# Two units of scores, then two units of weighing V, on TensorE

## The chip, the core and the metric

The kernel runs on one core of one Trainium2 chip. The metric is the device time in microseconds; before the change the median of three runs is 332.66 us (327.57 to 334.11).

## The reference

A gated cross-attention block followed by a gated feed-forward block with low-rank experts, in float32, on 32 images (batch entries) of 128 rows and width 128:

```
q = layernorm(x) * 8**-0.5;  k, v = split(ctx_2048, 2)       # 16 heads of 8
w = softmax(q @ k.T + b + mask(seq_len))                     # 128 x 128 per head
x = x + tanh(g_xattn) * (w @ v)
h = layernorm(x)
gate_e = (times e is in the top 2) * (sum of the top 2 scores)
x = x + tanh(g_ffn) * sum_e gate_e * (relu(h @ wi.T + bi + (h @ A_e.T) @ B_e.T) @ wo.T + bo)
```

The change concerns the attention alone. What has to be done there for each image: the scores of 16 heads, the row maxima, the exponentials, and the weighing of V with the sums of the rows.

## The kernel before

**Units.** An image's 16 heads are four units of four heads (c = 0 to 3). The scores are computed twice. First with queries as rows (line 779), so that VectorE can reduce them to negated row maxima (row_max, line 1040). Then with keys as rows (line 785), where the negated maximum comes in as one more row of the contraction, so that ScalarE can take the exponential of what is in the bank (exps, line 594). Q and K are split into bfloat16 parts which lie, with bias and maximum rows, in a tensor called stack, 64 partitions for each half of the heads. A call scores(m, n, c) issues four matmuls of each kind, interleaved, on different halves of the array: first-kind scores of image m, second-kind scores of image n.

**The pipeline.** All four engines run a loop over q (turns, or pairs of images), i (0 or 1) and c. At a turn, m = 2q+i and n = 2(q-2)+i: the second scores are four images behind the first. weigh_v (line 807) multiplies V by the probabilities in float32, four heads in four column groups of 32 of the array, eight matmul records a unit; behind(j) calls it for unit j. Its output bank o_acc is copied out by ScalarE (copy_o, line 600) when an image's four units are done, transposed by TensorE (transpose_o, line 817), and normalised and added to X by VectorE (add_attention, lines 1076 to 1089).

**The maxima.** The 32 columns of negated maxima of a pair are split on VectorE into three bfloat16 parts (split_max, lines 1054 to 1063, in four steps), transposed (transpose_max, 795), copied by ScalarE (copy_max, 606) and written to the stack by a DMA that ScalarE issues (max_to_stack, 611). The pair's second scores begin in the turn after the one that transposes them.

**Q and K of the pair q+3.** GpSimd permutes K (446) and normalises X (456); TensorE transposes both into one bank (transpose_k 751, transpose_q 756); ScalarE makes the first part (first_part, 579) and a float copy (float_copy, 583); GpSimd takes the rest (480); ScalarE makes the second part (second_part, 587); GpSimd the third (484); SyncE's DMAs bring them to the stack.

**What sets the order.** Each engine's order is written out by hand; semaphores join them. The waits that matter here:

```
scores:   pe.wait_ge(s_max, i - 1)       # two banks of first scores
scores:   pe.wait_ge(s_maxrow[p % 4], ...)   # line 773, first unit of a pair: the maxima's DMA
scores:   pe.wait_ge(s_exp, k - 1)       # two banks of second scores
weigh_v:  pe.wait_ge(s_oc, n)            # line 803, c == 0: copy_o of image n-1
weigh_v:  pe.wait_ge(s_exp, i + 1)
copy_o:   act.wait_ge(s_pv, CH * (n + 1))    # all four units of image n weighed
exps:     act.wait_ge(s_pv, i - 3)       # four buffers of probabilities
```

In the turns from q=13 to 15 the place of Q and K is taken by transposes and copies of the weights (lines 731 to 741, 569, 572). From q=16 there are only second scores; the layer norms of the feed-forward part (normalise(g), line 620, four activations each) and its gates run between them. Then comes the feed-forward stage, one group of four images at a time.

Of the kernel before, what the change touches and what calls it, by code (L numbers as in the profile page):

```python
# [39 lines left out]
def flamingo(nc, x, ctx, seq_len, g_xattn, g_ffn, b, wi, bi, wo, bo, lora_a, lora_b, gate_w, gate_b, out):  # L40
    B, S, D = x.shape
# [5 lines left out]
    PAIRS = B // 2  # L47
# [4 lines left out]
    CH = 4  # L52
# [7 lines left out]
    with es:  # L60
# [184 lines left out]
        LEAD = 4  # L245
# [313 lines left out]
        def _(act):  # L559
# [21 lines left out]
            def float_copy(p):  # L581
                act.wait_ge(s_rest, p)
                act.activation(full[:, :], qk_t[:, :], ACT.Copy).then_inc(s_full, 1)  # L583
# [5 lines left out]
            def exps(n, c):  # L589
                i = CH * n + c  # L590
                act.wait_ge(s_sc2, i + 1)
                if i >= 4:
                    act.wait_ge(s_pv, i - 3)
                act.activation(probs[:, i % 4, :], sc2[i % 2][:, :], ACT.Exp).then_inc(s_exp, 1)  # L594
# [7 lines left out]
            def copy_max(p):  # L602
                act.wait_ge(s_mT, p + 1)
                if p >= 2:
                    act.wait_ge(s_maxrow[(p - 2) % 4], 16 * ((p - 2) // 4 + 1))
                act.activation(max_rows[:, p % 2, :], bank_max[:, 0:256], ACT.Copy).then_inc(s_mTc, 1)

            def max_to_stack(p):
                act.wait_ge(s_mTc, p + 1)
                c0 = 256 * (p % 2)  # L610
                act.dma_start(stack[MAX_ROW:MAX_ROW + STEP * (ROWS - 1) + 1:STEP, (p // 2) % SLOTS, :, c0:c0 + 256],
                              max_rows[:, p % 2, :]).then_inc(s_maxrow[p % 4], 16)
# [47 lines left out]
            for q in range(PAIRS + 3):  # L660
                for i in range(2):
                    n = 2 * (q - 2) + i
                    for c in range(CH):
                        if 0 <= n < B:
                            exps(n, c)
                        if c == 1 and 0 <= n - 1 < B:
                            copy_o(n - 1)
                        if i == 0:
                            if c == 2 and LEAD <= q + 3 < PAIRS:
                                first_part(q + 3)  # L670
                            if c == 3 and 0 <= q - 1 < PAIRS:
                                copy_max(q - 1)
                            if c == 3 and LEAD <= q + 3 < PAIRS:
                                float_copy(q + 3)
                        else:
                            if c == 0 and 0 <= q - 1 < PAIRS:
                                max_to_stack(q - 1)
                            if c == 2 and LEAD <= q + 3 < PAIRS:
                                second_part(q + 3)
                        if c == 3 and 0 <= 2 * (q - WEIGHTS_AT) + i < 4:  # L680
                            copy_weights(2 * (q - WEIGHTS_AT) + i)

                        at = (q - PAIRS, i, c)
                        if at == (0, 0, 3):
                            normalise(0)
                        if at == (0, 1, 2):
                            copy_xT(0)
                        if at == (1, 0, 0):
                            gate_exp(0)
                        if at == (1, 0, 1):  # L690
                            normalise(1)
                        if at == (1, 1, 1):
                            copy_xT(1)
                        if at == (1, 1, 2):
                            x_high(0)
                        if at == (2, 0, 1):
                            normalise(2)
# [22 lines left out]
        def _(pe):  # L720
# [23 lines left out]
            def transpose_k(p):  # L744
                pe.wait_ge(s_kperm, 2 * (p + 1))
                if p > LEAD:
                    pe.wait_ge(s_full, p - LEAD)
                elif p >= 1:
                    pe.wait_ge(s_rest, p)
                for i in range(2):  # L750
                    pe.transpose(qk_t[:, 256 + i * 128:256 + (i + 1) * 128], kperm[:, p % 2, i, :], ident[:, :])  # L751
# [7 lines left out]
            def scores(m, n, c):  # L759

                first, second = 0 <= m < B, 0 <= n < B
                if first:
                    i, Q, s = CH * m + c, m // 4, (m // 4) % SLOTS
                    if c == 0 and m % 4 == 0:
                        pe.wait_ge(s_stack[s], 16 * STACK_DMAS * (Q // SLOTS + 1))
                        if Q < SLOTS:
                            pe.wait_ge(s_fixed[s], 32)
                    if i >= 2:
                        pe.wait_ge(s_max, i - 1)
                if second:  # L770
                    k, p = CH * n + c, n // 2
                    if c == 0 and n % 2 == 0:
                        pe.wait_ge(s_maxrow[p % 4], 16 * (p // 4 + 1))
                    if k >= 2:
                        pe.wait_ge(s_exp, k - 1)
                for j in range(G):
                    if first:
                        (at, h0), q0 = score_rows(UNITS1[c]), (m % 4) * 128
                        mm = pe.matmul(sc1[i % 2][:, j * 128:(j + 1) * 128], stack[at, s, h0 + j, q0:q0 + 128],  # L779
                                       stack[at, s, h0 + j, 512 + q0:640 + q0], start=True, stop=True)  # L780
                        if j == G - 1:
                            mm.then_inc(s_sc1, 1)
                    if second:
                        (at, h0), q0, t = score_rows(UNITS2[c]), (n % 4) * 128, (n // 4) % SLOTS
                        mm = pe.matmul(sc2[k % 2][:, j * 128:(j + 1) * 128], stack[at, t, h0 + j, 512 + q0:640 + q0],  # L785
                                       stack[at, t, h0 + j, q0:q0 + 128], start=True, stop=True)
                        if j == G - 1:
                            mm.then_inc(s_sc2, 1)

            def transpose_max(p):  # L790
                pe.wait_ge(s_msplit, NMS * (p + 1))
                if p >= 1:
                    pe.wait_ge(s_mTc, p)
                for i in range(2):
                    mm = pe.transpose(bank_max[:, i * 128:(i + 1) * 128], max_part[:, p % 2, i, :], identb[:, :])  # L795
                mm.then_inc(s_mT, 1)
# [15 lines left out]
            def transpose_o(n):  # L812
                pe.wait_ge(s_oc, n + 1)
                if n >= 1:
                    pe.wait_ge(s_norm, NNORM * (n - 1) + 4)
                for i in range(2):
                    mm = pe.transpose(o_t[:, i * 128:(i + 1) * 128], o_rows[:, n % 2, i * 128:(i + 1) * 128], ident[:, :])  # L817
                mm.then_inc(s_oT, 1)
# [77 lines left out]
            def behind(j):  # L896
                if 0 <= j < CH * B:
                    weigh_v(j // CH, j % CH)
# [5 lines left out]
            for q in range(PAIRS + 3):  # L904
                for i in range(2):
                    m, n = 2 * q + i, 2 * (q - 2) + i
                    for c in range(CH):
                        if c == 3:
                            behind(CH * n)
                        scores(m, n, c)  # L910
                        if i == 0:
                            if c == 0 and LEAD <= q + 3 < PAIRS:
                                transpose_k(q + 3)
                            if c == 2 and LEAD <= q + 3 < PAIRS:
                                transpose_q(q + 3)
                        if c == 3 and 0 <= n - 1 < B:
                            transpose_o(n - 1)

                        if c != 2:
                            behind(CH * n + c - 2)  # L920
                        if i == 0 and c == 1 and 0 <= q - 1 < PAIRS:
                            transpose_max(q - 1)
                        if c == 2 and 0 <= 2 * (q - WEIGHTS_AT) + i < 5:
                            transpose_weights(2 * (q - WEIGHTS_AT) + i)

                        at = (q - PAIRS, i, c)
                        if at == (0, 1, 1):
                            transpose_x(0)
                        if at == (0, 1, 3):
                            lora_and_gates(0)  # L930
                        if at == (1, 1, 0):
                            transpose_x(1)
# [411 lines left out]
```

## Time and profile before

| | |
|---|---|
| median of three runs | 332.66 us |
| the profiled execution | 328.71 us, span 326.8 us |
| TensorE busy | 260.8 us (80%) |
| VectorE busy | 236.8 us (72%) |
| ScalarE busy | 165.1 us (51%) |
| GpSimd busy | 124.1 us (38%) |
| mean granted clock of TensorE | 0.963 |
| the chain that ended last, by engine | PE 34%, issue 20%, DVE 20%, DMA 10% |

PE is TensorE, DVE VectorE, ACT ScalarE, POOL GpSimd, SP SyncE. The attention loop with both kinds of scores runs from about 43 to 182 us, the feed-forward stage from about 207 us to the end. A granted clock of 1.00 is 2.4 GHz, 0.50 is 1.2 GHz.

### The profile page before, as it was taken

The numbers are of one execution on the slowest core, as the hardware profiler recorded it, in microseconds if no ns is written. First come the engines' busy times: TensorE is split into PE (matmuls) and PEld (weight loads), VectorE is DVE, ScalarE is ACT, GpSimd is POOL, SyncE is SP. The second block draws the span as 40 slices with busy tenths as digits, with TensorE's granted clock in tenths as the row PEclk, the third lists the DMA queues.
The fourth block names the chain that finished last, engine by engine and source line by source line (L and its number), as shares of the span: only waits on it lengthen the run. The fifth ranks groups of instructions, "written<-read, shape, count | busy, mean of one in ns | idle before, by whom it ended". The sixth has DMA issues, their size and how long they took to land.

```text
span 326.8 us, 8070 instructions
## 1 busy us (share of the span) xinstructions
PE 260.8 (80%) x2934; PEld 179.0 (55%) x2934; DVE 236.8 (72%) x810; ACT 165.1 (51%) x332; POOL 124.1 (38%) x240
## 2 busy tenths in 40 slices
PE   0222058979879698889899886999999999999894
PEld 0111034444445344445455454878888888888764
DVE  1862078788969678869988778688797978867431
ACT  1230004767858577768776886444443445333230
POOL 9963005465536656534211412050504325033120
PEclk9999999997979869979999998799999999999999
DMA  6789980874908479682600000001010100101011
GB/s 172 141 181 189 233 155 10 197 143 106 231 12 227 78 181 193 117 168 62 165 9 4 19 2 1 2 1 32 2 32 2 33 10 24 32 2 34 0 34 32
DMA packets 36615, 26.70 MB, mean 82 GB/s; under 512 B 7992, under 2 KB 34400, under 8 KB 36576
## 3 DMA queue, kind: packets, MB, share of 16 engines
q1 hardware_dynamic: 33792, 25.12, 34.9%
q10 hardware_dynamic: 2784, 1.07, 1.5%
q8 instruction: 24, 0.39, 0.5%
q14 instruction: 15, 0.12, 0.2%
HBM read 7.25 MB, written 2.10 MB: 29 GB/s over the span
## 4 chain that ended last, share of the span: by engine, by line
PE 34%; issue 20%; DVE 20%; DMA 10%; POOL 7%; SPq 6%; ACT 3%; ACTq 0%; DVEq 0%; POOLq 0%
DVE negmax L1040 10%; PE bank L861 8%; PE bank L779 7%; PE bank L807 6%; DMA stack<-max_rows 5%; PE bank_max L892 5%; DMA b_rows<-in_L_xattn_b_dram 2%; POOL rstd L493 2%; POOL x_part L497 2%; DMA X<-in_x_dram 2%; POOL base L509 2%; PE bank L756 1%; PE bank L817 1%; PE bank_max L795 1%; SPq L331 1%
## 5 line engine op out<-in xcount | busy, mean ns | idle before, releaser
L1040 DVE TENSOR_REDUCE negmax<-bank 128x4 f32<-128x512 f32 x128 | 86.7, 681 | 25.2 <-PE bank L779 24.0
L594 ACT ACTIVATE probs<-bank 128x512 f32<-128x512 f32 x128 | 75.6, 602 | 38.6 <-PE bank L785 37.9
L779 PE MATMUL bank<-stack 64*128 64x128 bf16 x512 | 56.2, 240 | 32.6 <-DVE negmax L1040 17.2
L779 PEld LDWEIGHTS bank<-stack 64*128 64x128 bf16 x512 | 32.3, 103 | 60.6 <-DVE negmax L1040 27.5
L807 PE MATMUL bank<-probs,vpad 128*32 128x128 f32 x1024 | 57.7, 300 | 4.8 <-issue 3.2
L785 PE MATMUL bank<-stack 64*128 64x128 bf16 x512 | 54.1, 230 | 0.5 <-ACT probs L594 0.5
L861 PE MATMUL bank<-u_part,b_part 128*128 128x512 f32 x192 | 52.0, 399 | 0.1
L652 ACT ACTIVATE h<-bank,bi_col 128x512 f32<-128x512 f32 x32 | 22.0, 688 | 45.4 <-PE bank L861 45.4
L861 PEld LDWEIGHTS bank<-u_part,b_part 128*128 128x128 f32 x192 | 35.5, 188 | 8.6 <-ACT h L652 0.5
L807 PEld LDWEIGHTS bank<-probs,vpad 128*32 128x32 f32 x1024 | 21.3, 111 | 24.1 <-issue 16.2
L785 PEld LDWEIGHTS bank<-stack 64*128 64x128 bf16 x512 | 30.6, 99 | 3.5 <-issue 2.0
L892 PE MATMUL bank_max<-woT,hsum 128*128 128x128 f32 x256 | 30.7, 278 | 2.1 <-DVE hsum L1194 1.7
L493 POOL TENSOR_TENSOR rstd<-veps,half_neg 128x4 f32<-128x4 f32 x8 | 8.1, 1017 | 63.8 <-DVE veps L1103 63.8
L892 PEld LDWEIGHTS bank_max<-woT,hsum 128*128 128x128 f32 x256 | 29.2, 192 | 4.1 <-DVE hsum L1194 4.0
L1194 DVE SCALAR_TENSOR_TENSOR hsum<-bank,nbi_col,h 128x512 f32<-128x512 f32 x32 | 23.4, 743 | 10.6 <-PE bank L861 10.6
L861 PE MATMUL bank<-x_part,wi_part 128*128 128x512 f32 x96 | 29.4, 415 | 0.3 <-DVE hsum L1194 0.3
L480 POOL TENSOR_TENSOR rest<-full,part 128x512 f32<-128x512 f32 x12 | 13.9, 1155 | 36.7 <-ACT full L583 36.7
L579 ACT ACTIVATE part<-bank 128x512 bf16<-128x512 f32 x16 | 9.5, 594 | 30.0 <-PE bank L756 30.0
L471 POOL COPY vpad<-KV 128x96 f32<-128x96 f32 x32 | 8.6, 268 | 38.5 <-PE bank L807 38.5
L751 PE MATMUL bank<-ident,kperm 128*128 128x128 f32 x32 | 8.9, 370 | 15.5 <-POOL kperm L446 8.8
L456 POOL TENSOR_SCALAR xhat<-X,qmul,qadd 128x128 f32<-128x128 f32 x32 | 18.1, 574 | 4.0 <-DVE qadd L984 3.9
L861 PEld LDWEIGHTS bank<-x_part,wi_part 128*128 128x128 f32 x96 | 16.9, 193 | 4.2 <-DVE hsum L1194 1.6
(121 smaller groups left out, 409.0 us busy)
## 6 DMA issues: line engine op xcount, KB each, us to landing
stack<-part SPq DMA_DIRECT2D x64, 128.0 KB, 3.5
KV<-in_ctx_dram SPq DMA_DIRECT2D x8, 512.0 KB, 5.5
stack<-part SPq DMA_DIRECT2D x16, 256.0 KB, 3.8
X<-in_x_dram SPq DMA_DIRECT2D x8, 256.0 KB, 5.8
out_dram<-res SPq DMA_DIRECT2D x8, 256.0 KB, 2.3
stack<-onesb SPq DMA_DIRECT2D x8, 128.0 KB, 5.9
stack<-zerosb SPq DMA_DIRECT2D x8, 128.0 KB, 5.0
stack<-bias_line SPq DMA_DIRECT2D x8, 128.0 KB, 5.1
```

The source lines that it names most:

```text
L456: pool.tensor_scalar(xhat[:, p % 2, i, :].rearrange("p (a d h) -> p a d h", a=2, d=DH), X[:, 2 * p + i, :].rearrange("p (a h d) -> p a d h ...
L480: pool.tensor_tensor(halves(rest), halves(full), pair_cols(part[0], p), ALU.subtract).then_inc(s_rest, 1)
L493: pool.tensor_tensor(rstd2[:, :], veps2[:, :], half_neg[:, 0:GT], ALU.pow).then_inc(s_pow2, 1)
L594: act.activation(probs[:, i % 4, :], sc2[i % 2][:, :], ACT.Exp).then_inc(s_exp, 1)
L652: act.activation(h1[:, c, :], chunk_bank(i)[:, :], ACT.Relu, bias=bi_col[:, c:c + 1]).then_inc(s_h1, 1)
L779: mm = pe.matmul(sc1[i % 2][:, j * 128:(j + 1) * 128], stack[at, s, h0 + j, q0:q0 + 128], stack[at, s, h0 + j, 512 + q0:640 + q0], start=T ...
L785: mm = pe.matmul(sc2[k % 2][:, j * 128:(j + 1) * 128], stack[at, t, h0 + j, 512 + q0:640 + q0], stack[at, t, h0 + j, q0:q0 + 128], start=T ...
L807: mm = pe.matmul(o_acc[32 * j:32 * j + 32, c0:c0 + 128], v_window(n, UNITS2[c], j), probs[:, i % 4, j * 128:(j + 1) * 128], start=(c in (0 ...
L861: mm = pe.matmul(dst, w[a], v[b], start=(start and k == 0), stop=(closed or (stop and k == 2)), skip_group_check=closed)
L892: mm = pe.matmul(bank_out[:, t * 128:(t + 1) * 128], hsum[:, c, t * 128:(t + 1) * 128], woT[:, c, :], start=(c == 0), stop=(c == FC - 1))
L1040: dve.tensor_reduce(negmax[:, p % 2, n % 2, u * G:(u + 1) * G], bank_cols(sc1[i % 2]), AX.X, ALU.max, negate=True).then_inc(s_max, 1)
L1194: dve.scalar_tensor_tensor(out=hsum[:, c, :], in0=chunk_bank(i)[:, :], scalar=nbi_col[:, c:c + 1], in1=h1[:, c, :], op0=ALU.max, op1=ALU.a ...
```

## The change

On TensorE, the units of weighing stood one behind each call of scores (the call at c=2 had its unit in front of the call at c=3). After the change two follow the call at c=1 and two the call at c=3; the transposes come behind these. On ScalarE, copy_o and copy_max go to c=2, the DMA of the maxima to c=3 of the first image, first_part and float_copy to c=0 and second_part to c=3 of the second image. No instruction is added or taken away.

```diff
@@ scalar, for i, for c @@
                         if 0 <= n < B:
                             exps(n, c)
-                        if c == 1 and 0 <= n - 1 < B:
+                        if c == 2 and 0 <= n - 1 < B:
                             copy_o(n - 1)
                         if i == 0:
-                            if c == 2 and LEAD <= q + 3 < PAIRS:
+                            if c == 2 and 0 <= q - 1 < PAIRS:
+                                copy_max(q - 1)
+                            if c == 3 and 0 <= q - 1 < PAIRS:
+                                max_to_stack(q - 1)
+                        else:
+                            if c == 0 and LEAD <= q + 3 < PAIRS:
                                 first_part(q + 3)
-                            if c == 3 and 0 <= q - 1 < PAIRS:
-                                copy_max(q - 1)
+                                float_copy(q + 3)
                             if c == 3 and LEAD <= q + 3 < PAIRS:
-                                float_copy(q + 3)
-                        else:
-                            if c == 0 and 0 <= q - 1 < PAIRS:
-                                max_to_stack(q - 1)
-                            if c == 2 and LEAD <= q + 3 < PAIRS:
                                 second_part(q + 3)
@@ tensor, for i, for c @@
+                        scores(m, n, c)
+                        if c == 1:
+                            behind(CH * n - 2)
+                            behind(CH * n - 1)
+                            if i == 0 and 0 <= q - 1 < PAIRS:
+                                transpose_max(q - 1)
+                            if i == 0 and LEAD <= q + 3 < PAIRS:
+                                transpose_k(q + 3)
                         if c == 3:
                             behind(CH * n)
-                        scores(m, n, c)
-                        if i == 0:
-                            if c == 0 and LEAD <= q + 3 < PAIRS:
-                                transpose_k(q + 3)
-                            if c == 2 and LEAD <= q + 3 < PAIRS:
+                            behind(CH * n + 1)
+                            if 0 <= n - 1 < B:
+                                transpose_o(n - 1)
+                            if i == 0 and LEAD <= q + 3 < PAIRS:
                                 transpose_q(q + 3)
-                        if c == 3 and 0 <= n - 1 < B:
-                            transpose_o(n - 1)
-
-                        if c != 2:
-                            behind(CH * n + c - 2)
-                        if i == 0 and c == 1 and 0 <= q - 1 < PAIRS:
-                            transpose_max(q - 1)
```

## Rows read from the trace of the kernel before

**Rows 1.** Windows: length, busy us (count) by engine, PEclk, DMA share, GB/s.
```profile
63.13:156.86 93.73, 80.31 (x1384) 42.99 (x1381) 78.37 (x248) 67.86 (x141) 51.02 (x99) 0.91 0.67 144
156.86:181.95 25.09, 22.99 (x424) 13.32 (x425) 21.92 (x69) 18.64 (x39) 5.34 (x15) 1.00 0.17 43
121.57:129.18 7.61, 7.29 (x138) 4.03 (x138) 7.28 (x22) 6.65 (x14) 4.59 (x11) 1.00 0.97 230
```
**Rows 2.** Chain that ended last, 62 to 182 us: start, us, what.
```profile
137.74 2.03 issue
```
**Rows 3.** Line 611, the DMA of the maxima.
```profile
DMA to landing us min/median/max: 2.0/3.4/5.2
```
**Rows 4.** Timeline of TensorE, one pair: start, us, what, [idle before].
```profile
130.05 0.21 PE L779 MATMUL bank<-stack 64*128 64x128 bf16 x1 [0.80 <-DMA stack<-max_rows]
...
131.10 0.23 PE L779 MATMUL bank<-stack 64*128 64x128 bf16 x1
...
131.43 0.43 PE L807 MATMUL bank<-probs,vpad 128*32 128x128 f32 x8
131.79 0.28 PE L795 MATMUL bank_max<-identb,max_part 128*128 128x128 bf16 x2
...
134.12 0.23 PE L779 MATMUL bank<-stack 64*128 64x128 bf16 x1
...
136.25 0.43 PE L807 MATMUL bank<-probs,vpad 128*32 128x128 f32 x8 [0.32 <-issue]
...
137.30 0.43 PE L807 MATMUL bank<-probs,vpad 128*32 128x128 f32 x8
```
**Rows 5.** Timeline of ScalarE in the same pair (ACTq: its DMA queue).
```profile
131.57 0.60 ACT L594 ACTIVATE probs<-bank 128x512 f32<-128x512 f32 x1 [0.47 <-PE bank L785]
...
132.97 0.59 ACT L579 ACTIVATE part<-bank 128x512 bf16<-128x512 f32 x1
...
134.02 0.38 ACT L606 ACTIVATE max_rows<-bank_max 128x256 bf16<-128x256 bf16 x1
134.29 0.60 ACT L583 ACTIVATE full<-bank 128x512 f32<-128x512 f32 x1
134.59 0.55 ACTq L611 DMA_DIRECT2D stack<-max_rows  x1
134.76 1.10 ACT L594 ACTIVATE probs<-bank 128x512 f32<-128x512 f32 x2
135.76 0.39 ACT L600 ACTIVATE o_rows<-bank 128x256 f32<-128x256 f32 x1
```
**Rows 6.** Timeline of VectorE in the same pair.
```profile
130.47 0.69 DVE L1040 TENSOR_REDUCE negmax<-bank 128x4 f32<-128x512 f32 x1 [0.53 <-PE bank L779]
...
131.51 0.19 DVE L1063 TENSOR_TENSOR max_part<-max_rest,max_part 128x32 bf16<-128x32 f32 x1
```
**Rows 7.** Timeline of TensorE where two units of weighing touch.
```profile
199.20 0.65 PE L807 MATMUL bank<-probs,vpad 128*32 128x128 f32 x16
```
**Rows 8.** Windows around one stall, TensorE only: length, busy us, PEclk.
```profile
90.00:92.00 2.00, 0.34 (x14) 1.00 0.11 24
92.00:94.00 2.00, 2.00 (x26) 0.50 0.00 0
```
**Rows 9.** Chain that ended last, at the low clock.
```profile
117.45 0.58 PE bank L807 x8
...
118.57 0.58 PE bank L807 x8
```
**Rows 10.** Timeline of ScalarE and TensorE in the last turns.
```profile
193.04 0.38 ACT L600 ACTIVATE o_rows<-bank 128x256 f32<-128x256 f32 x1
...
194.85 1.67 ACT L594 ACTIVATE probs<-bank 128x512 f32<-128x512 f32 x3
...
201.72 1.65 ACT L620 ACTIVATE xhat<-X,nmean,rstd 128x128 f32<-128x128 f32 x4 [0.76 <-DVE nmean L1107]
...
202.40 0.45 PE L817 MATMUL bank<-ident,o_rows 128*128 128x128 f32 x1 [1.89 <-DVE o_norm L1083]
```

## The prediction

> **What bounds the kernel now.** I read the windows first, then the chain of waits, then the timeline of single pairs. "Pair" is one turn of q. "S0" to "S3" are a turn's calls of scores, "W" one unit of weighing, "e0" to "e3" the exponentials.
>
> The ten pairs from 63.13 to 156.86 us take 93.73 us, 9.37 each; the three up to 181.95, in which no Q and K are prepared, take 25.09, 8.36 each [rows 1]. A pair in which nothing was late takes 7.61 us, with TensorE 7.29 and VectorE 7.28 busy. So about 1.8 us of an average pair is waiting and slow clock, not work.
>
> The chain shows where: at the edge between pairs it stands on the DMA that carries the row maxima into the stack, as the 2.03 us up to 139.77 which the chain calls "issue", since nothing is on record for them [rows 2]. Line 773 makes S0 wait for that DMA. It is issued at 134.59, 4.54 us after its pair's S0 (130.05) [rows 4, 5], and these DMAs land in 2.0 to 5.2 us [rows 3]. 4.54+5.2 = 9.7 is the pair from 130.05 to 139.77. A stall costs twice. After one with 1.66 us idle of 2.00 the granted clock is 0.50 [rows 8], TensorE's lower level of 1.2 GHz; there a unit of scores and weighing takes 1.12 us, 117.45 to 118.57 [rows 9], instead of 0.69.
>
> **The change: what it removes.** First, switches of the array. Today every S is followed by something else; the pitch is 0.33 from S to W (131.10 to 131.43) and 0.36 from W onward (131.43 to 131.79) [rows 4]. Two W with nothing between take 0.65 for sixteen matmuls, against 0.43 for eight [rows 7], so W to W costs 0.22. S to S isn't in the trace: between that 0.22 and 0.33; I take 0.22, as W is the nearest row. Two units then need 0.22+0.33+0.22+0.36 = 1.13 instead of 1.38, or 1.0 us a pair on TensorE alone, 16 us over sixteen pairs. The Trainium skill (TensorEngine Tiling, Key Properties) says that changing the tiling mode drains the engine, and by that rule those 16 us are the gain and the time 328.7-16 = 313. The rows agree that a switch costs 0.11 to 0.14; whether the time comes back depends on what follows.
>
> Second, the maxima's DMA leaves earlier: copy_max is in front of e3 instead of behind first_part and e3. Third, first_part and float_copy (about 0.5 each) come some 2.4 us later, in the second image. GpSimd's subtraction waits for float_copy, and place_v is queued behind it; the weighing that needs this V comes only in the next pair, some 5 us after. SyncE's DMAs of the parts start as much later and are needed a whole pair after. I cost these at 0; if that cover went, S0 of every second pair would be late by up to 2.4.
>
> **What it adds: a chain through copy_o.** W of the next unit (weighing c=0) waits for copy_o (line 803), since both use the same bank. copy_o moves from behind e1 to behind e2, and e2 needs S2. Today W0 starts 0.10 after copy_o in second images, and behind transpose_q without waiting in first ones. In the changed order only S3 lies between S2 and W0. The links: S to exponential 0.47 (131.10 to 131.57); one exponential to the next 0.50; copy_o 0.39; to W 0.10 (135.76+0.39 to 136.25) [rows 4, 5]. So W0 can't start before S2+0.47+0.50+0.39+0.10 = S2+1.46. From W0 on: W 0.22, W 0.36, transpose_o 0.36 (136.25 to 137.30 is W, S and transpose_o), 0.94 to the next S0, with transpose_q (0.36) 1.30.
>
> *First image of a pair.* S0 at 0. Row_max starts at 0.42 and the last step of split_max ends 1.23 later (130.47 to 131.51+0.19) [rows 6], so transpose_max starts at 1.75, 0.09 after it [rows 4]; TensorE was ready at 1.13 and idles 0.6. It takes 0.22 (its 0.28 less the 0.07 by which a group overlaps the next), transpose_k 0.36 (130.05 to 131.10 is S, transpose_k and W) [rows 4]. S2 is at 2.34, W0 at 3.80 (idle 0.8 since S3), the next S0 at 5.10. Today: 130.05 to 134.12, 4.07.
>
> *Second image.* ScalarE takes e0 at 0.47, first_part 0.97, float_copy 1.52 (first_part and one exponential take 1.05: 132.97 to 134.02), e1 2.00 (float_copy to exponential 0.47), e2 2.50, copy_o 3.00 to 3.39, W0 3.49, next S0 4.43 [rows 5]. S3 needs e1's end and comes at about 2.7, TensorE idle for about 1.0 before it. Today's second image, TensorE alone, is 134.12 to 137.30+0.36 = 3.54 [rows 4].
>
> A pair is 5.10+4.43 = 9.53. The maxima: copy_max at 3.58, the issue at 4.15 (0.57 behind it, as 134.02 to 134.59 [rows 5]), landing at 9.35 at the latest; the stall is covered by the longer chain. If that cover went, it would return up to its old size. Ten pairs: 10 x (9.53-9.37) = **+1.6**.
>
> *The three later pairs* have no first_part and float_copy, but weight copies and transposes: S2 at 1.97, W0 3.43, S0 4.37; then S2 at about 1.4, W0 2.86, S0 3.80. A few copies of weights on ScalarE are covered by its waits. 8.17 against 8.36: **-0.6**.
>
> *Behind them.* Without a row_max the chain costs one image 0.3. In turn q=17 normalise(1) comes in front of e2 and copy_o. Today copy_o starts at 193.04, ahead of it, and e2, for which the next S0 waits, runs from 194.85 to 195.45 [rows 10]; in the new order copy_o starts 1.54 (normalise, its 1.65 less an overlap of 0.11) and 0.50 (e2) later, 195.1, W0 is at 195.6 and the next S0 at 196.5: 1.0. The last copy_o now stands behind normalise(2), which waits for VectorE until 201.72 and lasts 1.65 [rows 10]; the last transpose_o, at 202.40 today, comes at 201.72+1.65+0.38 = 203.75, 1.35 later, and transpose_u behind it. **+2.65** together, handed on whole to the feed-forward stage, which starts behind it and isn't touched. The first three turns: cold clock in both, 0 with 0.5 each way.
>
> **Sum**: 328.7 (the profiled execution; 326.8 is its span) +1.6-0.6+2.65 = 332.35. The profiled run is 4 us under the median of 332.66. I don't add these 4: if runs differ by when the maxima land, as I think, the new order hides that. The bounds: W to W or S to S at the full 0.36 and 0.33 adds 0.14 twice a pair, +4.5 in sixteen; if TensorE finds split_max done at 1.13, -0.6 a pair, -8 in thirteen. Forecast **332.5**.
>
> **Rivals.**
> *A, the switches were the bound (faster).* If copy_o weren't late and DMAs don't stall, pairs fall toward today's undisturbed 7.61, ten times -1.76, and the tail adds 2.6: 314. Halfway, with the stalls gone and the chain half hidden, 323. For it: TensorE 7.29 of 7.61 busy, the 0.11 to 0.14 a switch. Against: line 803 is a hard wait and S2+1.46 is made of measured links. 0.17.
> *B, the clock falls (slower).* The new order leaves TensorE idle in gaps of 0.5 to 1.1 us four times a pair, some 30% of it. Today an idle 0.80 (at 130.05) brought no fall, the 1.66 did [rows 4, 8]. The gaps lie between. A pair at the low level is 8 x 1.12 and five transposes, 1.66 x 1.12/0.69 = 2.7: 11.7, so +2.2. It decides where over a quarter of the pairs' time is low; a third of thirteen pairs is +9.5, 342, all of them 361. 0.28.
> *C, a late gap in my schedule*: place_v or VectorE's extra steps (0.54 for one X update) put 0.3 on each half: 16 x 0.6, 342. 0.1.
> The forecast itself, within some 4 us: 0.45.
>
> **The numbers.** Range 321 to 347: from half of A, past the forecast's +4.5 and C, to half of B. What a measurement can tell from no change is about 2%, 326.0 to 339.3. Faster: A, 0.17. Slower: most of B and C, 0.35. Within: 0.48.
>
> **What would show it.** In the changed profile: the waits of TensorE on the maxima's DMA gone; a wait of W on copy_o, 0.3 to 0.8 each image, in its place; S3 of second images waiting for e1; transpose_max waiting about 0.6; pair length 9.5; the last transpose_o near 205. If pairs are under 9 us, the chain through copy_o is wrong; if the granted clock in 63 to 157 is under its 0.91, B; if DMA waits stay, their issue wasn't early enough.

## The result: slower by 4.4%, and the profile after

The median is 345.53 us (four runs, 341.94 to 347.22) against 331.02 of the kernel before; the ratio is 1.044, with a 95% interval of 1.026 to 1.062. Here and below a median is over all runs, while a ratio compares only the runs of both kernels that were in the faster of two states. The forecast was 332.5.

The profiled execution after took 343.9 us (span 342.0), 15.2 more than that of before. First the windows of the changed kernel, turn by turn from q=3 to q=12, then the three turns to q=15; the columns are those of [rows 1].

```profile
63.91:75.73 11.82, 6.44 (x139) 4.32 (x139) 9.41 (x27) 6.56 (x14) 7.11 (x12) 0.97 0.93 196
75.73:86.74 11.01, 9.86 (x138) 6.60 (x139) 7.88 (x27) 6.60 (x14) 4.42 (x10) 0.57 0.17 44
86.74:98.52 11.78, 6.44 (x141) 4.31 (x140) 10.22 (x28) 6.55 (x14) 6.79 (x13) 1.00 0.95 198
98.52:109.25 10.73, 8.85 (x139) 5.87 (x140) 7.88 (x25) 6.55 (x14) 3.10 (x7) 0.68 0.17 45
109.25:120.02 10.77, 6.43 (x140) 4.33 (x139) 9.91 (x28) 6.56 (x14) 5.84 (x11) 0.97 0.93 190
120.02:131.03 11.01, 9.90 (x139) 6.63 (x140) 7.73 (x26) 6.62 (x14) 5.64 (x11) 0.56 0.17 45
131.03:142.42 11.39, 6.43 (x139) 4.33 (x139) 7.76 (x22) 6.57 (x15) 6.76 (x13) 1.00 1.04 214
142.42:153.24 10.82, 8.71 (x138) 5.81 (x139) 7.52 (x22) 6.55 (x14) 3.11 (x7) 0.68 0.50 95
153.24:162.62 9.38, 6.36 (x139) 4.31 (x139) 7.70 (x22) 6.55 (x14) 4.90 (x10) 1.00 0.81 163
162.62:171.74 9.12, 6.36 (x139) 4.31 (x139) 7.44 (x22) 6.55 (x14) 3.20 (x6) 1.00 0.20 52
...
171.74:196.48 24.74, 21.12 (x425) 14.19 (x425) 21.11 (x68) 18.46 (x39) 6.25 (x15) 1.00 0.25 59
63.91:171.74 107.83, 75.76 (x1381) 50.82 (x1381) 83.43 (x246) 65.68 (x140) 50.89 (x98) 0.84 0.60 126
```

The ten turns take 107.83 us where before had 93.73 [rows 1]: 14.1 of the 15.2 are here. TensorE's busy time at the full clock fell from 7.29 a pair to 6.36, so the saved switches are real, and worth 0.9; but the turns are longer. Two patterns: the even turns of the first eight rows (second, fourth and so on) run at a mean clock of 0.56 to 0.68, and the odd turn in front of each is long, since its row includes the wait at the edge. The waits of the same stretch say on what (engine, line, waited for: us, times, longest):

```profile
PE bank L806 <- issue: 10.4, 20, 0.8
...
PE bank L778 <- ACT probs L594: 8.6, 10, 1.1
PE bank_max L794 <- DVE max_part L1062: 6.0, 7, 1.3
...
PE bank L778 <- DMA stack<-part: 4.2, 2, 2.4
...
PE bank L778 <- DMA stack<-max_rows: 2.8, 2, 1.9
```

Lines 778, 794 and 806 are 779, 795 and 807 of before. The first three rows are the waits that the prediction drew: W0 on copy_o (called "issue", as the trace has no event for it; e1 will confirm it), S3 on the exponential of c=1, transpose_max on split_max. The last two are stalls on DMAs, which the prediction had at nothing. In all they are no longer than in the kernel before, 7.0 us against 8.4, but they now come on top of longer turns. Its ten turns waited so (the second row is the stall of [rows 2]):

```profile
PE bank L779 <- DMA stack<-max_rows: 6.4, 4, 2.3
...
PE bank L779 <- issue: 2.0, 1, 2.0
```

New is the wait for the parts. The chain of waits from 64 to 172 us shows the four DMAs behind the stalls.

```profile
69.03 6.66 DMA stack<-part
...
91.89 6.58 DMA stack<-part
113.77 6.00 DMA stack<-max_rows
135.17 7.00 DMA stack<-max_rows
```

All four end at the start of an even turn. Two are the last DMA of Q's and K's parts, which ended no stall before; two are the maxima's. These leave about when the prediction said (4.5 and 4.1 us after their turn's begin, forecast 4.15), but now land in up to 7.0 us (5.2 before [rows 3]). The parts' DMAs are under way then, and behind 135.17 also those of the feed-forward weights; the runs don't tell which of them slows the maxima. SyncE's queue shows how late the parts' DMAs start. First the kernel before, in the turn that began at 111.05; then the changed one, in the turn that began at 75.73:

```profile
115.24 0.56 SPq L328 DMA_DIRECT2D stack<-part  x1
...
123.29 1.53 SPq L331 DMA_DIRECT2D stack<-part  x1
```
```profile
83.96 0.56 SPq L328 DMA_DIRECT2D stack<-part  x1
...
91.89 0.60 SPq L331 DMA_DIRECT2D stack<-part  x1
```

The first issue is 4.2 us after the turn's begin before and 8.2 after, the last 12.2 and 16.2. They are done 98.5-75.7 = 22.8 us after the turn's begin, where two turns of the forecast last 19.

### The profile page after: what moved, and what is told of

It is laid out like the page before. It is cut to its first block, busy times and chain, and to the rows that moved or that the text cites. A ratio compares the mean times of both kernels' runs of the same rounds, so it can differ in the third digit from the quotient of the medians.

```text
span 342.0 us, 8070 instructions
## 1 busy us (share of the span) xinstructions
PE 251.8 (74%) x2934; PEld 187.9 (55%) x2934; DVE 239.8 (70%) x810; ACT 162.3 (47%) x332; POOL 124.7 (36%) x240
## 3 DMA queue, kind: packets, MB, share of 16 engines
q10 hardware_dynamic: 2784, 1.07, 1.5%
## 4 chain that ended last, share of the span: by engine, by line
PE 32%; issue 23%; DVE 12%; DMA 11%; SPq 10%; POOL 6%; ACT 4%; ACTq 0%; DVEq 0%; POOLq 0%
PE bank L860 7%; PE bank L806 5%; PE bank L778 5%; DVE negmax L1039 5%; PE bank_max L891 4%; DMA stack<-part 4%; DMA stack<-max_rows 4%; SPq L333 3%; SPq L331 2%; DMA b_rows<-in_L_xattn_b_dram 2%; PE bank L784 2%; PE bank L816 2%; POOL x_part L497 2%; ACT probs L594 2%; POOL rstd L493 2%
## 5 line engine op out<-in xcount | busy, mean ns | idle before, releaser
L594 ACT ACTIVATE probs<-bank 128x512 f32<-128x512 f32 x128 | 74.3, 606 | 56.4 <-PE bank L784 55.8
L778 PE MATMUL bank<-stack 64*128 64x128 bf16 x512 | 52.0, 248 | 40.0 <-DVE negmax L1039 16.4
L778 PEld LDWEIGHTS bank<-stack 64*128 64x128 bf16 x512 | 34.7, 107 | 59.3 <-DVE negmax L1039 35.7
L806 PE MATMUL bank<-probs,vpad 128*32 128x128 f32 x1024 | 47.8, 311 | 15.8 <-issue 15.3
L784 PE MATMUL bank<-stack 64*128 64x128 bf16 x512 | 48.6, 240 | 0.3 <-ACT probs L594 0.2
L806 PEld LDWEIGHTS bank<-probs,vpad 128*32 128x32 f32 x1024 | 28.4, 120 | 25.6 <-issue 22.9
L784 PEld LDWEIGHTS bank<-stack 64*128 64x128 bf16 x512 | 32.2, 105 | 2.4 <-ACT probs L594 1.5
L471 POOL COPY vpad<-KV 128x96 f32<-128x96 f32 x32 | 9.4, 292 | 25.6 <-PE bank L806 25.4
L606 ACT ACTIVATE max_rows<-bank_max 128x256 bf16<-128x256 bf16 x16 | 6.2, 390 | 26.0 <-PE bank_max L794 26.0
```

Source lines behind the costliest of these rows:

```text
L806: mm = pe.matmul(o_acc[32 * j:32 * j + 32, c0:c0 + 128], v_window(n, UNITS2[c], j), probs[:, i % 4, j * 128:(j + 1) * 128], start=(c in (0 ...
```

## The experiments

Every experiment only changes an order that is written by hand; nothing is left out of the computation. The numbers are the median and the ratio to the kernel before, run beside it, with its 95% interval. Where two experiments are compared in percent, it is the difference of their ratios, in percent of the time before.

| | grouping | maxima early | copy_o late | Q, K late | K, V load late | us | ratio |
|---|---|---|---|---|---|---|---|
| the change | x | x | x | x | | 345.5 | 1.044 (1.026 to 1.062) |
| e1 | x | x | | x | | 336.1 | 1.014 (1.004 to 1.023) |
| e2 | x | x | x | | | 331.8 | 1.007 (1.001 to 1.014) |
| e3 | x | x | | | | 327.8 | 0.988 (0.985 to 0.992) |
| e4 | | x | | | | 329.8 | 0.993 (0.988 to 0.998) |
| e5 | x | x | x | x | x | 339.2 | 1.019 (1.008 to 1.030) |
| e6 | x | x | | | x | 321.5 | 0.966 (0.956 to 0.976) |
| e7 | | x | | only ScalarE's part | | 341.6 | 1.028 (1.019 to 1.038) |
| e8 | x | | | only TensorE's part | | 337.3 | 1.015 (1.004 to 1.026) |
| e9 | | x | | | x | 325.0 | 0.978 (0.971 to 0.984) |
| e10 | x | x | x | | x | 326.7 | 0.976 (0.967 to 0.985) |
| e11 | x | x | | x | x | 330.5 | 0.990 (0.986 to 0.995) |
| e12 | x | x | and split_max at once | | x | 317.6 | 0.954 (0.948 to 0.960) |

(e12 has copy_o in its old place.)

### e1: copy_o back

```diff
-                        if c == 2 and 0 <= n - 1 < B:
+                        if c == 1 and 0 <= n - 1 < B:
                             copy_o(n - 1)
```

> The changed kernel with copy_o back behind the exponential of c=1; all else as changed. In the changed kernel a pair of the ten takes 10.78 us: 9.53 of my schedule, about 0.7 of stalls of the first scores of even turns on the DMAs of Q's and K's parts, the rest clock and transpose_max. Theory 1 (late parts: first_part and float_copy in the second image start these DMAs some 4 us later, and every second pair waits for them): W0 comes 0.9 and 0.4 us earlier in the two images, but the stall grows by what the pairs lose, so only a part comes back: 334 to 341 us, stalls on the parts' DMAs over 8 us in total. Theory 2 (the chain through copy_o is most of the loss): 1.3 us a pair in thirteen and 1 to 2 us behind them, 324 to 329 us.

Measured 336.06, in the range of theory 1. The waits of TensorE from 63 to 172 us:

```profile
PE bank L778 <- ACT probs L594: 10.0, 11, 1.1
PE bank_max L794 <- DVE max_part L1062: 7.7, 7, 1.3
PE bank L778 <- DMA stack<-part: 7.3, 3, 3.4
PE bank L778 <- DMA stack<-max_rows: 4.4, 2, 2.9
```

W0's wait is gone from the list, and the two DMA waits rose from 7.0 to 11.7 us: a part of the time that the chain through copy_o had cost had covered the late landings, and comes back as stalls.

### e2 and e3: Q and K back, without and with copy_o

```diff
 # scalar, i == 0: c == 2: copy_max, then
+                                first_part(q + 3)
 # c == 3: max_to_stack, then
+                                float_copy(q + 3)
 # scalar, i == 1
-                            if c == 0 ...: first_part(q + 3); float_copy(q + 3)
-                            if c == 3 ...: second_part(q + 3)
+                            if c == 2 ...: second_part(q + 3)
 # tensor: transpose_k(q + 3) right behind scores c == 0, transpose_q(q + 3) behind c == 2
```

> The changed kernel with everything of Q and K back in its old place: transpose_k behind the scores of c=0, transpose_q behind those of c=2, first_part at c=2 and float_copy at c=3 of the first image, second_part at c=2 of the second. copy_o stays behind the exponential of c=2, the maxima's DMA stays early. Theory 1 (late parts): stalls on the parts' DMAs vanish (7 us), the low clock behind them too (3 us), and the second image sheds the 1.0 us that its exponential of c=1 waited for first_part and float_copy; the maxima's DMA then ends pairs at 9.2 or so: 327 to 334 us. Theory 2 (copy_o's chain): W0 still waits for copy_o, only the second images get shorter: 335 to 340. Theory 3 (the clock falls by the small gaps of TensorE as such): the mean clock of the ten pairs stays near 0.84 with no stall over 1.5 us left, 338 or more.

> Both together: the grouping of two scores and two weighings and the early DMA of the maxima are all that is left of the change. Theory 1 and 2: every price is gone; pairs are held by VectorE (7.3 busy) or by the maxima's DMA, 8.2 to 8.9 us: 319 to 327. If grouping as such costs something (the scores of c=1 must wait for row_max while weighings stand ready behind them), it is 0.1 a unit at most, and the result is that of e4 or up to 5 us above it. If the saved switches of the array are worth their 1 us a pair, it is below e4 by up to 10.

e2 gave 331.84, as theory 1 had it, e3 327.78, just above its range. Late Q and K cost 2.5% (e1 against e3), late copy_o 1.9% (e2 against e3), both 5.6%. So these two moves together are the whole slowdown. What e3 still waits for:

```profile
PE bank L779 <- DMA stack<-part: 11.1, 4, 4.0
```

So the parts' DMAs bound even turns as soon as the turns get shorter, although they leave early here. With 1.2 us for the maxima that is 12.3 us of stalls on DMAs, no less than the 11.7 of e1, where Q and K are late. What late Q and K add between e3 and e1 is S3's wait for the exponential of c=1 (0.6 to 10.0 us) and a longer wait of transpose_max (4.4 to 7.7).

### e4: only the maxima early

```diff
                         if i == 0:
+                            if c == 2 and 0 <= q - 1 < PAIRS:
+                                copy_max(q - 1)
                             if c == 2 and LEAD <= q + 3 < PAIRS:
                                 first_part(q + 3)
                             if c == 3 and 0 <= q - 1 < PAIRS:
-                                copy_max(q - 1)
+                                max_to_stack(q - 1)
```

> The kernel before with one thing of the change: copy_max in front of first_part at c=2 and its DMA at c=3 of the first image. TensorE's order is untouched. The DMA leaves about 1.0 us earlier in each pair. If the maxima's DMA bounds the kernel before, as read from its chain, 1 us comes back where a pair stalls by that much (seven of ten pairs) and some low clock with it: 320 to 326 us. If the landing only gets slower, because it meets more of the parts' DMAs, no change.

329.81, a gain of 0.7% where I had expected 2 to 4. The slowest landing of the maxima went from 5.2 to 7.0 us, and in two of the five stalls the last DMA is now one of the parts': 5.3 us of waits for them, 4.8 for the maxima. Read from one chain, the maxima were the bound; they stood in front of a second bound of nearly the same length.

### e5 and e6: the 512 KB load out of the parts' way

```diff
                     part_to_stack(Q, 1)
                     part_to_stack(Q, 2)
+                    if Q + 2 < QUADS:
+                        load_kv(Q + 2)
 ...
                     part_to_stack(Q, 0)
-                    if Q + 2 < QUADS:
-                        load_kv(Q + 2)
 ...
-                if q == 9:
+                if q == 11:
                     load_weights()
```

> The changed kernel; only SyncE's queue differs: the 512 KB load of later K and V goes behind the second and third parts' DMAs instead of in front of them, and the weights are loaded in turn 11 instead of 9. It tells apart what the even turns wait for. If the parts' DMAs are late because they start late and queue behind 512 KB (theory 1), the stalls of 2.5, 1.9, 0.9 and 1.9 us at even turns shrink by 1 to 2 each and the low clock behind them goes: 334 to 340 us against 345.5. If they are late by their start alone, or if the small gaps of TensorE lower the clock, 343 to 347.

> The same edit of SyncE's queue on e3 (grouping, early maxima, copy_o and Q and K in their old places; 327.8 us). Its even turns start 2.6, 2.5, 2.0, 1.2 and 4.0 us late, 12 us in all. If the load in front of the parts makes these, half of it or more comes back, with some low clock: 316 to 323 us, the best version so far. If the landings only depend on how many bytes are under way, no change: 326 to 329.

Both came out as theory 1 had it: 339.24 and 321.53, 6.3 us less each. For e6 that is clear of the noise; the intervals of e5 and of the changed kernel still touch (1.008 to 1.030, 1.026 to 1.062). The edit also loads the weights two turns later, and the runs don't separate the two loads. The changed kernel's waits for DMAs in e5:

```profile
PE bank L778 <- DMA stack<-max_rows: 1.9, 1, 1.9
PE bank L778 <- DMA stack<-part: 1.5, 1, 1.5
```

3.4 us instead of 7.0. TensorE's waits for W0 and S3 are as in the changed kernel (10.1 and 8.9 us), and the ten turns take 104.67 instead of 107.83, 3.2 less for 3.6 us less of stalls. Their mean clock is still only 0.87 (0.84 in the changed kernel, 0.91 before). Two of them, neighbours:

```profile
85.43:96.36 10.93, 7.78 (x139) 5.31 (x138) 8.99 (x27) 6.55 (x14) 4.92 (x10) 0.84 0.96 205
96.36:106.19 9.83, 6.37 (x140) 4.32 (x140) 9.00 (x27) 6.55 (x14) 4.92 (x10) 1.00 0.24 59
```

The third number from the end is the granted clock. No late DMA stood at the begin of either turn. The first, an odd one, fell inside: its transpose_max waited for split_max, its W0 for copy_o, and the weighing behind them took 1.08 us; the second had the same two waits and kept the clock:

```profile
87.87 0.29 PE L794 MATMUL bank_max<-identb,max_part 128*128 128x128 bf16 x2 [1.24 <-DVE max_part L1062]
89.75 1.08 PE L806 MATMUL bank<-probs,vpad 128*32 128x128 f32 x16 [0.82 <-issue]
...
98.80 0.28 PE L794 MATMUL bank_max<-identb,max_part 128*128 128x128 bf16 x2 [1.24 <-DVE max_part L1062]
100.69 0.64 PE L806 MATMUL bank<-probs,vpad 128*32 128x128 f32 x16 [0.81 <-issue]
```

The pair of turns from 106.19 repeats this (10.93 us at 0.84, then 9.88 at 1.00). So removing late DMAs gave time back, but the clock can also fall at gaps of 1.24 and 0.82 us alone, which costs some 1.1 us each time. Why one turn falls and its neighbour doesn't stays open. It isn't the load of the DMAs, a share of 0.96 here against 0.24: the changed kernel's turn at 86.74 had 0.95 and gaps of 1.28 and 0.81, and kept 1.00.

### e7: late parts on the old order of TensorE

```diff
 # on top of e4
-                            (i == 0) first_part(q + 3) at c == 2, float_copy(q + 3) at c == 3
-                            (i == 1) second_part(q + 3) at c == 2
+                            (i == 1) first_part(q + 3), float_copy(q + 3) at c == 0
+                            (i == 1) second_part(q + 3) at c == 3
```

> The kernel before with TensorE's order untouched, the early maxima as in e4 (329.8 us), and only first_part and float_copy moved to c=0 and second_part to c=3 of the second image, as the change has them. No grouping, copy_o behind the exponential of c=1. If late parts are a price of their own (theory 1), it is what e1 costs above e3, 8 us: 335 to 340 us, with stalls at even turns on the parts' DMAs. If they cost only where the grouping has moved the transposes and lengthened the turns, 329 to 332.

341.57, above the range, against 329.81 of e4: 3.5%, with no grouping and copy_o in its old place. So late parts are a price of their own. Its waits from 63 to 172 us:

```profile
PE bank L806 <- issue: 10.0, 10, 1.1
PE bank L778 <- DMA stack<-part: 7.0, 3, 2.6
PE bank_max L794 <- DVE max_part L1062: 5.2, 7, 0.9
PE bank L778 <- DMA stack<-max_rows: 1.7, 1, 1.7
```

In most second images W0 waits 1.1 us (0.35 in e4), for the exponential of c=1 stands behind first_part and float_copy and copy_o behind that. Against e4 this wait grew from 2.8 to 10.0 us and that of transpose_max from 1.8 to 5.2. The stalls on DMAs did not grow, 8.7 us against 10.1; but the turns are 1.3 us longer (ten of them some 105.5 us against 92), and by the prediction's reasoning that would have covered the stalls, had the parts not left later as well. The mean clock of the ten turns is 0.87, in e4 0.94. The run doesn't say how the 3.5% divides between the longer row on ScalarE, the landings and the clock.

### e8: TensorE's half alone

The diff is that of TensorE in the section on the change; ScalarE's order is the one of before.

> TensorE's half of the change alone; ScalarE's order is that of before, so copy_o is behind the exponential of c=1. transpose_q is now behind the weighing of c=3, and first_part stands in front of the exponential of c=3 on ScalarE and waits for it, with copy_max and the maxima's DMA queued behind: the DMA leaves at about 5.5 us of the turn instead of 4.5 and the next even or odd turn waits for it. I expect 338 to 346 us: the grouping needed ScalarE's move, as the parts and the maxima then meet. If grouping alone is harmless, 326 to 331.

337.30, a little under the range. The grouping moves transpose_q behind the weighing of c=3, and with the old order of ScalarE this holds first_part, the exponential of c=3 and the maxima up. ScalarE's half was meant for that place of transpose_q, but it costs more than it saves: the whole change is at 1.044, TensorE's half alone at 1.015. e3 keeps transpose_q early instead.

### e9: what is grouping worth

The edit of e6 on e4, so without grouping.

> e4 (the order of before on TensorE, early maxima) with the edit of SyncE's queue of e6: the load of K and V behind the parts, the weights in turn 11. It differs from e6 only by the grouping. If grouping is worth its saved switches, 1 us a pair, e6 (321.5 us) is below this by 8 to 16: 330 or more. If, as the traces of e3 and e4 read, VectorE's row_max ends the wait either way and only the turns without Q and K gain (some 1 us in three), this gives 321 to 325 us.

324.98, at the edge of what a worthless grouping gives. Against e6 grouping is worth 1.2%, and between e4 and e3 0.4%, some 4 and 1.5 us, both with intervals that overlap: little or nothing, and not the 16 us of its switches.

### e10 and e11: each late move by itself

e10 is e6 with copy_o at c=2, e11 is e1 with the edit of e6.

> e6 with copy_o behind the exponential of c=2, as the change has it, and nothing else. The price of the chain S2, two ScalarE steps, copy_o, W0 by itself, with the parts early and few DMA stalls to hide it. By my schedule W0 comes 0.9 us later in first images and, with no first_part in front of its exponentials, about 0.8 in second ones, of which scores already waiting for row_max hide half: 0.7 to 1.0 us a pair in sixteen pairs and about 1 us behind them, 332 to 338 us. If the stalls still hide it, as they did in e2 against e3 (4 us), 324 to 327.

> e6 with Q and K's steps late, as the change has them (both transposes behind the weighings, first_part and float_copy at c=0 and second_part at c=3 of the second image), and copy_o behind the exponential of c=1. With e5, e6 and e10 it closes a square on one queue order: e6 321.5, copy_o late 326.7, both late 339.2. In the trace of e7 late parts have two prices: in each second image the weighing waits 1.13 us instead of 0.35, since the exponential of c=1 stands behind first_part and float_copy (10 pairs, 8 us), and stalls at even turns. If the two moves only add up, this gives 339.2-5.2 = 334. If the chain of the second image is the shared price (exponential of c=1, of c=2, copy_o in a row behind float_copy), it gives 328 to 332 and the joint price is more than the sum by 2 to 5 us.

e10 gave 326.69, 1.0% above e6, where I had expected 3 to 5%. In most turns of its trace W0 waits 0.34 and 0.43 us in the two images, but transpose_max waits 0.31 instead of 0.5 to 1.0. A first image waits for split_max anyway; a late W0 in the image in front of it takes the place of a part of that wait instead of adding to it. e11 gave 330.49, 2.4% above e6; both moves together (e5) 5.3%. So the joint price is 1.9% more than the sum here and 1.1% more with the old queue. The intervals are about 1% each, so that is likely, not shown. The traces make it plausible: with both, float_copy, the exponentials of c=1 and c=2 and copy_o are one row in front of W0.

### e12: a better version

```diff
-                        if i == 0 and c == 0 and 0 <= q - 1 < PAIRS:
-                            split_max(q - 1, 1) ... split_max(q - 1, 3)   # between, two steps of add_attention
-                        elif c < 3 and 0 <= o < B:
+                        if c < 3 and 0 <= o < B:
 ...
                         if i == 1 and c == 3 and 0 <= q < PAIRS:
-                            split_max(q, 0)
+                            for step in range(4):
+                                split_max(q, step)
```

> e6 with VectorE's four steps of split_max one behind the other at the end of a turn, instead of three of them behind the first row_max of the next. transpose_max waits 0.5 to 1.0 us in each turn of e6 for the last step; here it should be ready when TensorE comes to it, and the maxima's DMA leaves as much earlier. VectorE pays some 0.3 us a turn for steps that now wait for each other, partly in time that it waits at the turn's edge. If transpose_max's wait is on the path: 313 to 319 us. If row_max then bounds the turns, 320 to 323.

317.55, within the range: 4.6% under the kernel before. Of this 3.4% were there in e6; the 1.2% that this edit adds has intervals that overlap (0.948 to 0.960, 0.956 to 0.976). The wait of transpose_max went from 7.0 us in e6 to 2.4, and a part of it to row_max (1.3 in e6):

```profile
PE bank L779 <- DVE negmax L1040: 6.8, 16, 0.9
PE bank L779 <- DMA stack<-max_rows: 4.4, 3, 2.6
PE bank_max L795 <- DVE max_part L1063: 2.4, 6, 0.6
```

## Why the prediction was wrong, step by step

**The cover over the DMAs, costed at 0: wrong, and the largest term of the miss.** The ten turns were to cost 1.6 us more than before and cost 14.1. Of the 12.5 between, 7.0 are stalls on DMAs that the forecast held to be covered, and some 5.4 the clock, which was in no term of the sum. *The parts*, 4.2 us of stalls: the prediction put float_copy "some 2.4 us later" and took SyncE's DMAs to start "as much later" and to be "needed a whole pair after". The first one leaves 4.0 us later, 8.2 after its turn's begin and not 4.2+2.4 = 6.6; eleven issues of 0.6 us and more follow, some of which wait for second_part and GpSimd, with 512 KB of K and V in front of the last; the last land after 6.6 us, against a median of 3.5. *The maxima*, 2.8 us: issued as early as forecast, but they land in up to 7.0 us and not 5.2, so "the stall is covered by the longer chain" failed as well. The text named the price of the first, "S0 of every second pair would be late by up to 2.4", and gave it no chance: the even turns from q=4 to q=10 start 2.37, 1.85, 0.88 and 1.89 us late. e5 shows that the landings are what is waited for, since a change of SyncE's queue alone halves these stalls. e7 shows the cover gone without the rest of the change: its turns are 1.3 us longer than those of e4, and 8.7 us of stalls are left.

This is the miss against the forecast. Against the kernel before, whose turns also stalled, the changed one is slower since its turns without stalls are longer (9.1 to 9.9 us, where 7.61 was the undisturbed turn [rows 1]), as the forecast had it, and since this length didn't buy the stalls off.

**The length of a pair, 9.53: right on average.** Ten of them are 95.3 us; the 7.0 of stalls and the low clock of four turns (43.57 us for the four, 38.1 by schedule, so 5.4) make 107.8, which is the measured sum. Two errors offset each other in it: the odd turns up to the one at 131.03, less their stalls, took 9.45 to 9.93, as transpose_max waited 0.80 to 1.28 and not 0.6, and the last two turns 9.38 and 9.12. The turn at 162.62, at the full clock and without a late DMA, shows the steps (TensorE; of the scores only S3):

```profile
164.36 0.28 PE L794 MATMUL bank_max<-identb,max_part 128*128 128x128 bf16 x2 [0.55 <-DVE max_part L1062]
164.48 0.39 PE L750 MATMUL bank<-ident,kperm 128*128 128x128 f32 x2
166.24 0.65 PE L806 MATMUL bank<-probs,vpad 128*32 128x128 f32 x16 [0.81 <-issue]
166.81 0.44 PE L816 MATMUL bank<-ident,o_rows 128*128 128x128 f32 x2
167.09 0.38 PE L755 MATMUL bank<-ident,xhat 128*128 128x128 f32 x2
...
170.08 0.21 PE L778 MATMUL bank<-stack 64*128 64x128 bf16 x1 [1.07 <-ACT probs L594]
```

Forecast were 0.6 of wait for transpose_max (0.55), 0.8 for W0 (0.81) and about 1.0 for S3 (1.07). The turn took 9.12, less than 9.53, mostly since neighbouring transposes cost 0.12 to 0.32 rather than 0.22 and 0.36.

**The switches of the array: the size right, the gain mostly lost.** 6.36 busy instead of 7.29 [rows 1], 0.9 a pair for 1.0. By the Trainium skill (TensorEngine Tiling, Key Properties) a change of tiling mode drains the engine; the traces agree in so far as fewer changes make the same matmuls 0.9 us shorter, the drain itself they don't show. But e9 against e6 finds some 4 us of the 16, and e4 against e3 1.5, as VectorE and the DMAs then end the wait.

**The three later turns, -0.6:** 24.74 for 25.09, so -0.35. **The tail, +2.65:** from the begin of q=16 to the last transpose_o 21.54 (196.48 to 218.02) for 20.45 (181.95 to 202.40), +1.1. The first W0 of q=17 came 1.7 later against q=16's begin (13.3 behind it, 11.6 before), but the last copy_o didn't wait for normalise(2) as the sum had it; that one began 0.7 earlier against q=16's begin, and copy_o waited for the last weighing:

```profile
215.59 1.64 ACT L620 ACTIVATE xhat<-X,nmean,rstd 128x128 f32<-128x128 f32 x4
...
217.58 0.38 ACT L600 ACTIVATE o_rows<-bank 128x256 f32<-128x256 f32 x1 [0.35 <-PE bank L806]
```

**The first turns, 0 with 0.5 each way:** +0.8. The reason given, a cold clock in both, is a misreading: the granted clock is 1.00 in both up to 63 us. The rest of the span, the feed-forward stage with it, took 0.4 less.

**The 4 us between profile and median:** not added, in the belief that the new order hides late landings. It hides few of them: 7.0 us of stalls on DMAs are left of 8.4. The changed kernel's median is 1.6 us above its profile.

**Rival B, the clock by the small gaps: in part right.** The clock did fall, to 0.84 in the mean for 0.91. In the changed kernel's trace each fall comes with a late DMA: the turns at 153.24 and 162.62 have all the small gaps, up to 1.07 us, and no late DMA, and keep 1.00. At 118 to 120 us a stall of 0.88 behind gaps of 1.07 and 0.32 was enough for a fall, where before an idle 0.80 had brought none. But e5 had two falls with no late DMA ahead of them. And the falls are no more than before, four in each trace, while the time at 1.2 GHz doubled: from the mean clocks I estimate some 17 us of the ten turns before and 34 after. In e5, with half the stalls, it is still 27. What keeps the clock low for longer isn't shown; TensorE goes on idling in these turns, 0.61 us in front of the first W0 of each. How much of the 14 us is this rival's own stays open. A turn with a fallen clock took 10.9 on average (43.57/4), not 11.7.

**The range** (321 to 347) held the time, but the direction had only 0.35, and for other reasons.

## What to carry to other kernels

When a step is moved, follow what it starts to the last consumer with times from the trace, the issue times of the queue and the landings under load among them: "needed a whole pair after" isn't a cover until its slack is a number. A stage whose chain ends on one DMA may have a second one right behind it (e4), and only removing the first shows it. A longer turn doesn't cover a late transfer when the same move delays the transfer as well (e7). Saved time on the busiest engine comes back only as far as the next wait, here row_max and split_max on VectorE; the largest gain that is clear of noise (e6 over e3, 2.2%) came from reordering a queue, not from TensorE's work.

## What the runs showed of the hardware that I had not expected

A cast of 128x32 on VectorE takes 0.18 us when GpSimd is idle; beside a subtraction of GpSimd it lasted until that one ended, 1.11 to 1.17 us in five turns of the changed kernel:

```profile
46.95 0.18 DVE L1054 CAST max_part<-negmax 128x32 bf16<-128x32 f32 x1
```
```profile
86.80 1.16 POOL L484 TENSOR_TENSOR part<-rest,part 128x512 bf16<-128x512 f32 x1 [0.72 <-ACT part L587]
```
```profile
86.83 1.17 DVE L1053 CAST max_part<-negmax 128x32 bf16<-128x32 f32 x1
```

The first row is of the kernel before, the others of the changed one. In odd turns of the changed kernel this put transpose_max off by up to 1.3 us instead of 0.6; it is the wait that e12 shortens. Second, the landing of one 64 KB DMA ranged from 2.0 to 7.0 us with what else was under way, a wider spread than that of any compute instruction of the loop that I looked at (the cast above: 0.18 to 1.17).
